# Part of the last stage moved into attention, its loop reordered, the second bias summed on TensorE

## What is computed

```
x = x + conv_ref(ln_c(x), ...)      # attention with a relative bias per row and column
t = t + ffn_ref(ln_t(t), ...)
# conv_ref: softmax(q k / 4 + bias_h + bias_w) v, then out @ Wp + bp
# ln_t(v) = (v - mean) / sqrt(var + 1e-5) over the channels
# ffn_ref:
#   xq = round(clip(x0 / alpha_a1.mean(), -8, 7)); wq1, wq2 likewise per row
#   x1 = xq @ wq1.T * alpha_w1 * alpha_a1.mean() + b1
#   x1 = clip(gelu(x1), -10, 10)
#   hq = round(clip(x1 / alpha_a2.mean(), -8, 7))
#   x2 = hq @ wq2.T * alpha_w2 * alpha_a2.mean() + b2
```

## Time and profile before

| | |
|---|---|
| median of 3 runs | 881.89 us (879.38 to 884.87) |
| the profiled execution, its own time | 880.72 us |
| its span, first to last instruction | 878.9 us |
| TensorE busy | 775.8 us, 88% |
| VectorE busy | 696.7 us, 79% |
| ScalarE, GpSimd busy | 574.0 us, 447.7 us |
| mean granted clock of TensorE | 0.942 |
| phase "ff" on the timeline | 761.2 us to the end |

### The profile page before, as it was taken

The page is one execution under the profiler, slowest core; times in us unless marked ns, Lnnn a source line. Parts: engine busy times, 40 slices in busy tenths (PEclk is TensorE's granted clock), DMA queues, the critical chain, the costliest instruction groups (busy, mean ns, idle before and its releaser), DMA issues. The chain is left out here.

```text
span 878.9 us, 14775 instructions
## 1 busy us (share of the span) xinstructions
PE 775.8 (88%) x5656; PEld 404.5 (46%) x5656; DVE 696.7 (79%) x965; ACT 574.0 (65%) x969; POOL 447.7 (51%) x284
## 2 busy tenths in 40 slices
PE   4999456588999999999999999999999998678874
PEld 2655456243444444444444444444444441356653
DVE  6998844696888888888888888888888880179995
ACT  1343335136787778787878777787777878257673
POOL 3677796445373738474665748373734444012120
PEclk9999767679999999999999999999999999889986
DMA  7675599999977584939293949577690001333411
GB/s 195 214 223 192 177 286 363 311 184 184 155 151 163 123 186 95 203 76 213 69 209 68 222 82 201 107 158 151 132 178 13 13 1 34 116 132 102 145 37 54
DMA packets 65750, 130.02 MB, mean 148 GB/s; under 512 B 9535, under 2 KB 45392, under 8 KB 57224
## 3 DMA queue, kind: packets, MB, share of 16 engines
q1 hardware_dynamic: 57648, 115.95, 57.1%
q10 hardware_dynamic: 8032, 13.13, 4.3%
HBM read 89.73 MB, written 34.60 MB: 141 GB/s over the span
## 5 line engine op out<-in xcount | busy, mean ns | idle before, releaser
L1031 DVE TENSOR_REDUCE at_neg_max<-at_r_ps 128x1 f16<-128x1024 f32 x384 | 451.7, 1218 | 86.4 <-PE at_r_ps L903 86.4
L989 ACT ACTIVATE at_probs<-at_s_ps 128x512 f32<-128x512 f32 x768 | 410.8, 600 | 97.4 <-PE at_s_ps L923 96.5
L923 PE MATMUL at_s_ps<-op_mix_q,op_mix_k 128*128 128x512 f16 x768 | 264.3, 383 | 10.8 <-issue 3.9
L903 PE MATMUL at_r_ps<-op_mix_k,op_mix_q 128*128 128x256 f16 (+1 forms) x1920 | 239.9, 258 | 13.3 <-DMA op_mix_q<-bias_parts 8.6
L935 PE MATMUL at_o_ps<-at_probs,op_v_u 128*32 128x512 f32 x1536 | 204.1, 604 | 0.0
L903 PEld LDWEIGHTS at_r_ps<-op_mix_k,op_mix_q 128*128 128x128 f16 x1920 | 157.3, 100 | 91.3 <-DVE at_neg_max L1031 15.7
L822 POOL COPY op_mix_q<-op_mix_q 2x4096 f16<-2x4096 f16 x48 | 171.6, 3601 | 1.5
L923 PEld LDWEIGHTS at_s_ps<-op_mix_q,op_mix_k 128*128 128x128 f16 x768 | 73.8, 97 | 175.5 <-issue 74.4
L220 POOL MEMSET op_mix_q<- 2x10240 f32 x12 | 103.5, 8628 | 21.2 <-PE at_o_ps L935 21.1
L826 POOL TENSOR_TENSOR at_o_sb<-at_o_sb,at_inv_rows 128x512 f32<-128x512 f32 x24 | 30.7, 1279 | 141.1 <-DVE at_inv_rows L1047 139.9
L819 POOL COPY op_mix_q<-op_mix_q 2x1024 f16<-2x1024 f16 x24 | 24.9, 1036 | 113.0 <-ACT op_mix_q L994 113.0
(11 more groups left out here) (116 smaller groups left out, 655.2 us busy)
## 6 DMA issues: line engine op xcount, KB each, us to landing
op_mix_q<-qk_parts SPq DMA_DIRECT2D x48, 640.0 KB, 10.7
op_mix_q<-bias_parts SPq DMA_DIRECT2D x120, 120.0 KB, 9.6
op_mix_q<-bias_parts SPq DMA_DIRECT2D x72, 128.0 KB, 9.5
qk_parts<-op_mix_q SPq DMA_DIRECT2D x24, 256.0 KB, 2.4
v_rows<-pr_v_st SPq DMA_DIRECT2D x8, 768.0 KB, 4.1
op_mix_k<-qk_parts SPq DMA_DIRECT2D x48, 128.0 KB, 13.2
op_v_u<-v_rows SPq DMA_DIRECT2D x12, 512.0 KB, 13.9
op_mix_q<-bias_parts SPq DMA_DIRECT2D x24, 256.0 KB, 9.9
```

Source lines behind the costliest of these rows:

```text
L903: last = pe.matmul(r_ps[count % RRING][:, first // GROUP, first % GROUP:first % GROUP + n], mix_q[owner.buf][:, variant, j, qt * P:(qt + 1 ...
L923: pe.matmul(s_ps[use % SRING][:, :], mix_k[unit.buf][:, j, keys], mix_q[unit.buf][:, ops.VARIANT_OF[kt], j, queries], start=True, stop=Tru ...
L989: act.activation(probs[n % PRING][:, j, :], s_ps[use % SRING][:, :], ACT.Exp).then_inc(s_taken, 1)
L1031: dve.tensor_reduce(neg_max[half][:, j // 2, t, j % 2:j % 2 + 1], r_ps[count % RRING][:, :, :].rearrange("p h t -> p (h t)"), AX_X, ALU.ma ...
```

## The change

1. In phase "at", the last unit's steps 6 to 11 take two of group 0's twelve projection matmuls each, into the place of r_ps[0]. VectorE makes residual and normalising of group 0 at step 12, GpSimd the inverse deviation. The loads of the first bias and of groups 0 and 1, the identity and the constants move into unit 10. The buffers y (now four), y_n, y_r, y_q, the statistics and the identity move into the area of mix_q0.
2. The last half of attention's output is copied by ScalarE at the end of "at" and is inverted, multiplied and stored in "ff", at the head of the lists of VectorE, GpSimd and SP. SP waits there for all stores before its first load (group 2). The buffers of that half lie in those of y[2] and y[3].
3. The transposes of a group become a step `turn(g+1)` of their own, on TensorE between project(g+2) and second(g−1); ScalarE copies at the end of its turn.
4. The second bias is divided by s2_row in the setup chain, split into three bf16 rows, and summed by four more matmuls in `second` (a matrix of ones). y_b and `add_b2` go. The setup chain gets 12 instructions and one more row is loaded.
5. `normalise`: the factor inv_a1 is multiplied in by a third GpSimd operation; three rounding operations become two; a memset goes. `stage_c`: the four scalings become one instruction.

```diff
 class FfnInputs(Keep):
-    N_PARAMS = 3 + NH
+    N_PARAMS = 2 + NH
+    YRING = 4
...
+    def inverse_std(self, pool, g, inv_a1):
+        pool.wait_ge(self.aggr_done, g.n + 1)
+        pool.tensor_tensor(out=self.var_eps[g.s][:, :], in0=self.meanvar[g.s][:, :, 1], in1=self.eps[:, :], op=ALU.add).then_inc(self.eps_done, 1)
+        pool.wait_ge(self.eps_done, g.n + 1)
+        pool.tensor_tensor(out=self.rstd[g.s][:, 0, :], in0=self.var_eps[g.s][:, :], in1=self.half_neg[:, :], op=ALU.pow).then_inc(self.pow_done, 1)
+        pool.wait_ge(self.pow_done, g.n + 1)
+        pool.tensor_tensor(out=self.rstd[g.s][:, 3, :], in0=self.rstd[g.s][:, 0, :], in1=inv_a1.to_broadcast([P, TILES]), op=ALU.mult).then_inc(self.scaled_pow, 1)
...
+        dve.wait_ge(self.scaled_pow, g.n + 1)
+        dve.scalar_tensor_tensor(out=r1, in0=r2, scalar=1.5, in1=r3, op0=ALU.add, op1=ALU.mult).then_inc(self.newton, 1)
...
+        dve.tensor_scalar(self.y_r[:, :, :], self.y_n[:, :, :], MAGIC, MAGIC + QP, ALU.add, ALU.min).then_inc(self.yr_done, 1)
+        dve.wait_ge(self.yr_done, g.n + 1)
+        need(dve, self.t_done, g.n - 1)
+        dve.tensor_scalar(self.y_q[g.s][:, :, :], self.y_r[:, :, :], MAGIC + QN, -MAGIC, ALU.max, ALU.add).then_inc(self.yq_done, 1)
...
 phase_attention, gpsimd:
+                if unit.u == UNITS - 2:
+                    pool.wait_ge(pv_done, unit.u * STEPS)
+                    ffn_in.make_consts(pool)
...
             each_unit(pool, emit)
-            normalise(Unit(UNITS - 1, BATCH - 1, UNITS - 1), 1)
+            ffn_in.inverse_std(pool, FIRST, wt.inv_a1)
 sync:
+                if unit.u == UNITS - 2:
+                    sp.wait_ge(pv_done, unit.u * STEPS)
+                    for stored in o_stored:
+                        sp.wait_ge(stored, 16 * unit.u)
+                    ffn_in.load_biases(sp)
+                    ffn_in.load(sp, FIRST)
+                    ffn_in.load(sp, FIRST.after(1))
                 store(unit, 0)
...
 tensor:
+                        part = (n - PROJECT_FROM) * 2 + j // 2
+                        if unit.last and j % 2 == 0 and 0 <= part < len(PARTS):
+                            if part == 0:
+                                pe.wait_ge(ffn_in.params_in, 16 * ffn_in.N_PARAMS)
+                                pe.wait_ge(ffn_in.att_loaded[0], 16)
+                                pe.wait_ge(reduced, UNITS * ROWS)
+                            last = ffn_in.project_part(pe, FIRST, p_ps, *PARTS[part])
+                            if part == len(PARTS) - 1:
+                                last.then_inc(ffn_in.proj_done, 1)
...
 vector:
+                    if unit.last and n == HEAD_AT:
+                        ffn_in.residual(dve, FIRST, p_ps)
+                        ffn_in.normalise(dve, FIRST)
...
 Weights.scales:
+        link(dve.memset(self.b2_parts[:, :], 0.0))
+        link(dve.memset(self.ones[:, :], 1.0))
+        link(dve.reciprocal(self.inv_s2[:, :], self.s2_row[:, :]))
+        link(dve.tensor_tensor(self.b2_row[:, :], self.b2_row[:, :], self.inv_s2[:, :], ALU.mult))
+        for i in range(3):
+            row = slice(i * SLOT, i * SLOT + 1)
+            link(dve.tensor_scalar(self.b2_high[:, :], self.b2_row[:, :], 1.0, None, ALU.mult))
+            link(dve.tensor_scalar(self.b2_parts[row, :], self.b2_high[row, :], 1.0, None, ALU.mult))
+            if i < 2:
+                link(dve.tensor_tensor(self.b2_row[:, :], self.b2_row[:, :], self.b2_high[:, :], ALU.subtract))
...
 phase_ffn, sync:
+            sp.wait_ge(ffn_in.last_normed, 1)
+            sp.dma_start(att_dram[GROUPS - 1, :, NQUAD - 1, :], ffn_in.o_last[:, :]).then_inc(o_stored[1], 16)
+            for at in o_stored:
+                sp.wait_ge(at, 16 * UNITS)
...
 gpsimd:
+            pool.wait_ge(ffn_in.last_spread, 1)
+            pool.tensor_tensor(out=ffn_in.o_last[:, :], in0=ffn_in.o_last[:, :], in1=ffn_in.o_inv_rows[:, :], op=ALU.mult).then_inc(ffn_in.last_normed, 1)
+            ffn_in.inverse_std(pool, FIRST.after(1), wt.inv_a1)
...
 vector:
+            invert_last()
+            ffn_in.residual(dve, FIRST.after(1), p_ps)
...
                 stage_b(g, 0)
+                if g.first:
+                    dve.wait_ge(ffn_in.last_normed, 1)
+                    dve.wait_ge(o_stored[1], 16 * UNITS)
...
                 if not g.first:
                     stage_c(g.after(-1))
-                if not g.last:
-                    add_b2(g.after(1))
...
 tensor:
                 for t in range(TILES):
+                    pe.matmul(f_ps[:, t, 0:C], wt.ones[:, :], wt.b2_parts[:, :], start=True, stop=False)
                     for k in range(HT):
...
+            turn(FIRST)
             project(FIRST.after(1))
...
                 hidden(g)
                 if not (g.last or g.after(1).last):
                     project(g.after(2))
+                if not g.last:
+                    turn(g.after(1))
                 if not g.first:
                     second(g.after(-1))
```

More of the change, by code:

```diff
@@ L287, in load_wp, with make_consts, project_part @@
                 sp.dma_start(self.wp_sb[head * SLOT:head * SLOT + HD, quad, :], self.wp[r:r + HD, :]).then_inc(self.params_in, 16)
+    def make_consts(self, pool):
+        make_identity(pool, self.ident, self.zeroed, self.ident_made)
+        pool.memset(self.eps[:, :], 1e-5).then_inc(self.pool_consts, 1)
+        pool.memset(self.half_neg[:, :], -0.5).then_inc(self.pool_consts, 1)
+        pool.wait_ge(self.pool_consts, 2)
+    def project_part(self, pe, g, p_ps, t, quad):
+        return pe.matmul(p_ps[:, t, 0:C], self.att[g.s][:, quad, t * P:(t + 1) * P], self.wp_sb[:, quad, :],
+                         start=(quad == 0), stop=(quad == NQUAD - 1))
@@ new lines, in residual @@
+    def residual(self, dve, g, p_ps):
+        st, mv, y_g = self.stats[g.s], self.meanvar[g.s], self.y[g.n % self.YRING]
+        dve.wait_ge(self.x_loaded[g.s], (g.it + 1) * 16)
+        dve.wait_ge(self.proj_done, g.n + 1)
+        need(dve, self.res_done, g.n - self.YRING + 1)
+        dve.tensor_tensor(y_g[:, :, :], p_ps[:, :, 0:C], self.x_in[g.s][:, :, :], ALU.add).then_inc(self.y_done, 1)
+        dve.wait_ge(self.y_done, g.n + 1)
+        for t in range(TILES):
+            last = dve.bn_stats(st[:, t, :], y_g[:, t, :])
+        last.then_inc(self.stats_done, 1)
+        dve.wait_ge(self.stats_done, g.n + 1)
+        for t in range(TILES):
+            last = dve.bn_aggr(mv[:, t, :], st[:, t, :])
+        last.then_inc(self.aggr_done, 1)
@@ L756, in phase_attention @@
             ph.sem(n) for n in ("o_out", "sums_turned", "inv_done", "inv_spread", "norm_done"))
-        o_stored = [ph.sem(f"o_stored{i}") for i in range(2)]
+        o_stored = ffn_in.o_stored
         block = ph.block()
@@ L806, in max_rows @@
             return s_ps[use % SRING][:, :].bitcast(F16)[0:2, :].rearrange("p (g t) -> p g t", g=QUAD // 2)
+        p_ps = r_ps[0][:, :, :].rearrange("p h (t c) -> p (h t) c", c=256)
+        PROJECT_FROM, PARTS = TURN_AT[1], [(t, quad) for t in range(TILES) for quad in range(NQUAD)]
+        HEAD_AT = INVERT_AT[1] + 1
         SPREADS = ((0, 1), (1, 3), (3, 5))
@@ L881, in emit @@
                     ops.load_bias(sp, nxt.u, nxt.buf)
+                if unit.u == UNITS - 2:
[5 more added lines that the diff above has]
+                    ffn_in.load(sp, FIRST.after(1))
                 store(unit, 0)
             each_unit(sp, emit)
-            sp.wait_ge(o_stored[0], 16 * UNITS)
-            sp.wait_ge(o_stored[1], 16 * (UNITS - 1))
-            ffn_in.load_biases(sp)
-            ffn_in.load(sp, FIRST)
-            ffn_in.load(sp, FIRST.after(1))
-            store(Unit(UNITS - 1, BATCH - 1, UNITS - 1), 1)
-            for half in range(2):
-                sp.wait_ge(o_stored[half], 16 * UNITS)
         @block.tensor
@@ L1001, in take_out, with take_last_out @@
                 act.activation(o_sb[half][:, :], o_ps[:, :], ACT.Copy).then_inc(o_out, 1)
+            def take_last_out():
+                act.wait_ge(pv_done, UNITS * STEPS)
+                act.activation(ffn_in.o_last[:, :], o_ps[:, :], ACT.Copy).then_inc(ffn_in.last_out, 1)
             def emit(unit):
@@ L1018, in _ @@
             each_unit(act, emit)
-            take_out(Unit(UNITS - 1, BATCH - 1, UNITS - 1), 1)
+            take_last_out()
         @block.vector
@@ L1273, in _ @@
         def _(dve):
-            def residual(g):
-                st, mv, rs = stats[g.s], meanvar[g.s], rstd[g.s]
-                dve.wait_ge(x_loaded[g.s], (g.it + 1) * 16)
-                dve.wait_ge(proj_done, g.n + 1)
-                dve.tensor_tensor(y[g.s][:, :, :], p_ps[:, :, 0:C], x_in[g.s][:, :, :], ALU.add).then_inc(y_done, 1)
-                dve.wait_ge(y_done, g.n + 1)
-                for t in range(TILES):
-                    last = dve.bn_stats(st[:, t, :], y[g.s][:, t, :])
-                last.then_inc(stats_done, 1)
-                dve.wait_ge(stats_done, g.n + 1)
-                dve.memset(rs[:, 1, :], 0.0)
```

(12 more changed lines are left out.)

176 lines of the change are left out of this document (81 added, 95 removed).

## The result

The changed kernel took 860.62 us (median of 4 runs, 859.48 to 864.04) against 883.34 us for the kernel before beside it (4 runs, 879.38 to 884.87): a ratio of 0.976, 95% interval 0.9726 to 0.9795. In a second set it took 864.01 us (6 runs, 861.76 to 868.84), ratio 0.9806 (0.9776 to 0.9835). The gain was 22.7 us in the first set and 18.1 in the second, where 864.0 was forecast from 881.89, a gain of 17.9. The profiled execution has a span of 857.7 us against 878.9, so 21.2 us less; that of the second set has 860.2.

What follows compares the result with a forecast made beforehand. VectorE was taken to bound setup and loop, with a serial start of the last stage. Start and loop −23.8, end +2.3 and setup +4.2 gave −17.3 us from 880.72, so 863.4; forecast 864.0, own range 861 to 867.

Steps and rivals of the forecast that it cites:

- What bounds: Setup and feed-forward loop bound by VectorE; 22.9 us of one group's serial work where attention ends and the last stage begins.
- Setup, +4.2: Setup: twelve more chained VectorE instructions, reciprocal 1.1 us and eleven others 3.1, add 4.2 us; ends 3 and 7.7.
- the two rows: Setup: earlier profile's reciprocals, 0.166 us on 2 elements and 0.233 on 16, giving 1.1 us on 192.
- paid whole: Setup: no cover, since VectorE is full and engines behind keep step, so all +4.2 us reaches the total.
- Attention, +1.7: Last attention unit: twelve projection matmuls lengthen six steps from 2.46 to 2.75 us, +1.7; ends 0 and 4.1.
- Where the stages meet: Attention to last stage: group 0's hidden starts at 762.2, group 2's load lands at 768.0, group 2 is normalised at 780.3.
- The cost of a cold clock: Start of last stage: first projection at 6.28 us instead of 4.07; with a later group 2 load +4, 868; chance 0.08.
- The loop, 10.44 a group: Feed-forward loop: VectorE saves 1.67 us a group, giving 10.44; TensorE needs 10.2 and fits by 0.25.
- TensorE sets the loop: Feed-forward loop rival: TensorE or a hand-over makes it 11.0 us a group, +3, 867 us; chance 0.14.
- The end, +2.3: Last group: later hidden +2.0, four more matmuls +0.7, two last scalings give back 0.4; ends 1 and 4.
- Sum: Whole kernel: −23.8 + 2.3 + 4.2 = −17.3 us; span-based 863.4, forecast 864.0.

Runs made afterwards that it cites:

- an addition back: Changed kernel plus one further 128 x 768 VectorE addition a group, into a scratch tile, ahead of the second layer's scaling: 870.26 us, ratio 0.987.
- one chain: Kernels keeping the twelve added setup instructions once, like the changed kernel (860.62, again 864.01 us); without ten of them 857.63 us, with those ten twice 866.86 us.
- the run with the load first: Changed kernel with SyncE issuing group 2's loads at the head of the last stage, before its wait for the last normalise: 863.18 us, ratio 0.978.
- The experiment: Changed kernel with group 5's second layer again ahead of group 7's turn, in the last loop turn but one only: 862.02 us, ratio 0.977.
- the rows late: Changed kernel with the twelve bias-row instructions moved from setup into the last attention unit, bias loaded with the last stage's parameters: 856.08 us, ratio 0.970.
- all repairs: Changed kernel with bias rows made late, group 2 loaded first, last turn behind the second layer, group 7's second layer into p_ps: 852.24 us, ratio 0.966.

## Why the prediction was right, step by step

The forecast was a gain of 17.3 us in the span. It was 21.2 and 18.7 in the two profiles. That the first set gained more is in part luck of the execution: its profile lacks the early wait that the profile of the kernel before has with 3.90 us. The terms, one by one:

- **What bounds.** Right. Setup is paid, the start is serial, the loop is VectorE's (an addition back costs 0.87 a turn), and all three were read from the earlier trace rows.
- **Setup, +4.2.** The chain is 4.59 us long: the reciprocal took 1.35, between the 1.1 of the two rows and the 1.6 of the estimate from the Trainium skill (VectorE: DVE Perf Modes, the section on the fixed hardware budget); the other eleven 0.29 each with hand-over (I had 0.28). The next phase starts 4.2 to 5.8 us later in the eight profiles with one chain (4.85 in the first, 4.7 in the second). But the step "paid whole" was too strict: last copy less early wait gives 3.4 us for 4.2 of chain. Attention's first row doesn't give a figure: it came 2.7 us later than before in the second profile (166.45 for 163.72) and 6.9 later in the first (170.66), with waits for the bias transfers of 6.48 and 11.95 us instead of 8.56.
- **Attention, +1.7.** Mis-sized (+0.66): a step with two parts took 2.61, not 2.75, and the first parts fell into waits altogether. The last weighing moved by 0.66 us (from 752.07 to 754.40, of which 1.67 was there ahead of the first parts).
- **Where the stages meet.** Right to 0.5 us: hidden of group 0 at 762.71 (762.2 forecast), the load landed at 767.8 (768.0), TensorE waited 1.72 (2.3), group 2 was normalised at 780.1 (780.3). But the forecast ran the path through that load alone; VectorE's own list was as long to 0.24 us, as the run with the load first showed. The cost of a cold clock behind that wait, which I had priced for projection 1 alone, struck projection 2, in five of the eight profiles in which it waited for that load (5.8 us for 4.2).
- **The loop, 10.44 a group.** 10.40 in the ten profiles that leave the loop as it is. TensorE fits, with 0.2 us of waiting before each turn (I gave it 0.25). The rival "TensorE sets the loop" is what one gets when the turn stays behind the second layer: 11.27 (11.0 in the rival, 11.3 in the expectation).
- **The end, +2.3.** Mis-sized: +2.96. Hidden started 5.5 us behind the last rounding, where I took 4.6 with 5.3 at the latest, and it took 3.78 us where I took 3.48: both the transposes (1.09 for 0.61) and the second layer (4.5) were slow. My own terms for this step (4.6 for 1.8, less 4.45 for 3.48) give +1.8, not the +2.0 that I wrote. The experiment gives about 3 us for this one order.
- **Sum.** From the last copy to the end I had −23.2 us; it was −23.5 where projection 2 was fast and −22.2 where it was slow. Setup and attention: +5.9 forecast, +2.3 and +3.5 measured, and +4.1 for the mean last copy of the eight profiles with one chain (759.0, with a mean early wait of 3.9 us, as before). With like early waits (4.12 after, 3.90 before) the span fell by 18.7 us, 1.4 more than forecast; the first profile's 21.2 has an early wait of 0 in it. So the sum holds, and what it had too much is in setup and attention: the first parts of the projection fell into waits, and where the missing 0.8 us of the chain went, no profile shows.

## What to carry to other kernels

An order that frees the bounding engine in the loop must be judged again for the last turn, where its partner is missing: here one changed place in TensorE's order gave back about 3 us. Work that depends on nothing should be put where its engine is idle: the same chain cost about 3.4 us in setup and nothing that shows in the last attention unit, 13.9 us of which VectorE had free. And before a gain or loss of a few us is put down to an edit, compare stretches between fixed points of several profiles: one wait varied by 8 us between executions, more than most of the edits were worth.

## What the runs showed of the hardware

**VectorE beside GpSimd.** With the rows late, the end of the chain fell beside GpSimd's copies. VectorE and GpSimd there:

```profile
725.03 0.26 DVE L1267 TENSOR_SCALAR op_mix_q<-op_mix_q 128x192 bf16<-128x192 f32 x1
...
726.48 7.19 POOL L911 COPY op_mix_q<-op_mix_q 2x4096 f16<-2x4096 f16 x2
726.67 3.55 DVE L1267 TENSOR_SCALAR op_mix_q<-op_mix_q 128x192 bf16<-128x192 f32 x1
...
730.25 3.48 DVE L1268 TENSOR_SCALAR wt_b_parts<-op_mix_q 1x192 bf16<-1x192 bf16 x1
...
735.91 0.71 DVE L1141 STREAM_TRANSPOSE at_turned<-at_o_sb 128x512 f32<-128x512 f32 x1 [2.17 <-ACT at_o_sb L1101]
```

A cast of 128x192 that took 0.26 us in setup took 3.55, and one of a single row of 192 elements 3.48 instead of 0.20: each ends within 0.15 us of the end of one of GpSimd's two copies of 3.6 us. The same two took 3.55 and 3.48 us with all repairs. GpSimd's copies were hardly slower (7.19 us for the two, 7.15 in the kernel before). It cost nothing here, since 2.17 us of idle time were left behind it. The other way round, GpSimd's third small operation took 0.98 us in the loop, where it ended 0.06 us behind VectorE's addition of 797.08, and 0.20 in attention, at 748.61, where VectorE had only operations of 0.16 us. The Trainium skill (GPSIMD Engine Reference, Specifications) names SBUF interfaces shared by the two, with contention where VectorE runs in a two-port mode or reads two inputs from SBUF. The second reading agrees: that addition reads two tiles. Of the first one, the cast and the one-row copy read one tile each, and no trace here shows the mode in which they ran. In setup GpSimd did nothing from 35.9 to 45.9 us, so the chain met no such copy there.

**The clock after a short wait.** Projection 2 waited 1.68 to 1.85 us for its load in eight profiles. It took 4.17 us in three of them and 5.81 to 5.85 in the other five, and the length of the wait doesn't tell them apart (1.72, 1.72 and 1.80 in the fast ones, 1.68 to 1.85 in the slow ones). A window of 1 us inside it, in the first profile and in the second:

```profile
769.00:770.00 1.00, 1.00 (x8) 1.00 (x7) 0.93 (x3) 1.00 (x2) 0.00 (x0) 1.00 0.99 406
...
769.00:770.00 1.00, 0.99 (x3) 0.99 (x4) 1.00 (x4) 1.00 (x1) 0.00 (x0) 0.50 1.16 309
```

The granted clock is 1.00 in the fast one and 0.50 in the slow one, the lower of its two levels. Taking the wait away made it fast each time (4.07, three profiles). So a short wait can cost as much again through the clock, in some executions and not in others; what decides it is not shown.
